# The last stage of a transformer kernel as loops: both expert outputs added to the residual on VectorE

## The reference

```python
logits = jnp.einsum('sbd,de->sbe', x, Wg) + bg + bias
vals, idx = jax.lax.top_k(logits, TOP_K)          # TOP_K = 2
w = jax.nn.softmax(vals - jnp.max(vals, axis=-1, keepdims=True), axis=-1)
cw = jnp.einsum('sbk,sbke->sbe', w, jax.nn.one_hot(idx, NUM_EXPERTS, dtype=x.dtype))
h = jax.nn.relu(jnp.einsum('sbd,edh->esbh', x, W1) + b1[:, None, None, :])
y = jnp.einsum('esbh,ehd->esbd', h, W2) + b2[:, None, None, :]
out = jnp.einsum('esbd,sbe->sbd', y, cw)
...
x = x + _L1_ffn_ref(_layernorm(x, axis=-1), ...)
```

## Time and profile before

| | |
|---|---|
| median of 3 runs | 2008.19 us (2007.45 to 2008.85) |
| the profiled execution | 2008.85 us |
| its span, first to last instruction | 2007.1 us |
| busy, share of the span | PE 87%, DVE 64%, ACT 51%, POOL 23% |
| the edited stage, first load to last instruction | 1967.63 to 2007.1 us |
| loads and stores in it | 16 and 8 of 512 KB |
| the last store is issued at | 2003.76 us |

### The profile page before, as it was taken

How to read it: one execution, slowest core, us unless ns; L and a number is a source line. 1 busy time by engine, 2 the same in 40 slices (tenths; PEclk the granted TensorE clock), 3 DMA queues, 4 the chain that set the end, 5 groups by cost and what they waited for, 6 DMA issues and landing times. The chain is left out here.

```text
span 2007.1 us, 38130 instructions
## 1 busy us (share of the span) xinstructions
PE 1746.5 (87%) x10689; PEld 1076.5 (54%) x10690; DVE 1293.4 (64%) x2730; ACT 1016.1 (51%) x2046; POOL 458.4 (23%) x597
## 2 busy tenths in 40 slices
PE   6949999999999999998869986999978549999990
PEld 5802333233233233222758875989876249988880
DVE  7759888788788788871458868555546662222224
ACT  4614777667677677777235432344322225554442
POOL 4636000000000000000101224322122155555550
PEclk9957999999999999999879997999988759999995
DMA  4562221122221122200010001131311922222117
GB/s 152 162 149 32 33 33 33 35 33 33 35 33 33 35 33 33 33 1 1 0 12 1 0 11 44 44 84 42 85 43 51 339 91 66 65 65 65 63 63 259
DMA packets 119479, 121.80 MB, mean 61 GB/s; under 512 B 20692, under 2 KB 97512, under 8 KB 119208
## 3 DMA queue, kind: packets, MB, share of 16 engines
q1 hardware_dynamic: 106568, 94.35, 19.9%
q0 software_dynamic: 7584, 20.72, 3.2%
q10 hardware_dynamic: 5184, 4.98, 0.7%
HBM read 88.04 MB, written 31.59 MB: 60 GB/s over the span
## 5 line engine op out<-in xcount | busy, mean ns | idle before, releaser
L1873 DVE TENSOR_REDUCE mx<-ps 128x1 f32<-128x512 f32 x1024 | 634.9, 682 | 104.5 <-PE ps L2020 104.2
L1947 ACT ACTIVATE PR<-ps 128x512 f32<-128x512 f32 x1024 | 533.9, 607 | 189.5 <-PE ps L2081 186.1
L2020 PE MATMUL ps<-KQ 96*128 96x512 bf16 x1024 | 408.7, 405 | 34.2 <-PEq L210 25.3
L2081 PE MATMUL ps<-KQ 99*128 99x512 bf16 x1024 | 391.8, 389 | 18.5 <-issue 9.8
L2020 PEld LDWEIGHTS ps<-KQ 96*128 96x128 bf16 x1024 | 99.5, 99 | 360.0 <-DVE mx L1873 270.1
L2046 PE MATMUL ps<-PR,VO 128*32 128x512 f32 x2048 | 270.3, 606 | 0.0
L2081 PEld LDWEIGHTS ps<-KQ 99*128 99x128 bf16 x1024 | 99.7, 98 | 143.7 <-ACT PR L1947 59.2
L1968 POOL COPY VO<-V 128x512 f32 (+1 forms) x16 | 9.8, 615 | 719.8 <-PE ps L2046 719.6
L1746 PEld LDWEIGHTS ps<-e_xinT,e_w 128*128 128x128 f32 x1264 | 156.6, 195 | 5.8 <-issue 1.9
L1746 PE MATMUL ps<-e_xinT,e_w 128*128 128x128 f32 x1264 | 157.5, 279 | 1.1 <-ACT e_xinT L1678 1.1
L1736 PE MATMUL ps<-eW,e_hiddenT 128*128 x632 | 154.9, 388 | 3.1 <-issue 1.1
(11 more groups left out here) (289 smaller groups left out, 2354.0 us busy)
## 6 DMA issues: line engine op xcount, KB each, us to landing
KQ<-qk_parts SPq DMA_DIRECT2D x192, 128.0 KB, 4.7
TB<-toeplitz_lines SPq DMA_DIRECT2D x32, 512.0 KB, 5.9
qk_parts<-parts SPq DMA_DIRECT2D x8, 1536.0 KB, 6.8
eW<-in_L_ffn_W SPq DMA_DIRECT2D x16, 512.0 KB, 6.3
eW<-in_L_ffn_W SPq DMA_DIRECT2D x8, 1024.0 KB, 12.0
e_got<-expert_outputs SPq DMA_DIRECT2D x16, 512.0 KB, 9.7
X<-in_L_attn_x SPq DMA_DIRECT2D x8, 512.0 KB, 4.7
expert_inputs<-e_xn SPq DMA_DIRECT2D x8, 512.0 KB, 3.2
```

What stands on the lines that cost most here:

```text
L1873: nc.vector.reduce_max(mx[:, k, h, q:q + 1], ps[:, bank(r, ("max", t))], AX).then_inc(red_done, 1)
L1947: nc.scalar.activation(PR[:, kt % 2, h, qc * BANK:(qc + 1) * BANK], ps[:, st_bank(r, s)], ACT.Exp).then_inc(exp_done, 1)
L2020: nc.tensor.matmul(ps[:, bank(r, ("max", t))], KQ[r][0:KROWS, 1, h, q * P:(q + 1) * P], KQ[r][0:KROWS, 0, h, k * BANK:(k + 1) * BANK], sta ...
L2081: nc.tensor.matmul(ps[:, st_bank(r, s)], KQ[r][0:AROWS, 0, h, kt * P:(kt + 1) * P], KQ[r][0:AROWS, 1, h, qc * BANK:(qc + 1) * BANK], start ...
```

## The change

The stage's three lists become loops on the engines, and ScalarE no longer computes.

SyncE: a loop of two rounds with four chunks each. It first adds 32 to the semaphore `added`, so that each chunk can wait for a positive number. Each of its two loads (slot 0, then slot 1) has a row number worked out in the loop, and both raise the one semaphore of the buffer.

VectorE: the same loop. For each chunk it waits for its own adds of the chunk before, copies the chunk's 128 x 8 weights into a small buffer `w`, waits for the copy and for both loads, then does four scaled adds for slot 0, waits for these, and does four scaled adds for slot 1. Each add reads and writes the tile X[:, CT*c + k], and its address is worked out in the loop. The buffer `second`, the scalings and the wide add are gone.

ScalarE: a loop of eight rounds, each of which waits for a chunk's eight adds and issues its store.

```diff
@@ -1760,51 +1760,46 @@
         with ExitStack() as s2:
             LOADED = 4
             got = sbuf(s2, "e_got", [P, LOADED, 2, CT, D])
-            second = sbuf(s2, "e_second", [P, 2, CT, D])
-            loaded = [[sem(f"e_y_loaded{r}{s}") for s in range(2)] for r in range(LOADED)]
-            scaled, first_added, added, out_stored = (sem(n) for n in ("e_scaled", "e_first_added", "e_added", "out_stored"))
-            flat = lambda v: v.rearrange("p k d -> p (k d)")
+            w = sbuf(s2, "e_weight", [P, 2, 2, CT])
+            loaded = [sem(f"e_y_loaded{r}") for r in range(LOADED)]
+            load_turn, w_ready, added, out_turn, out_stored = (sem(n) for n in ("e_load_turn", "e_w_ready", "e_added", "out_turn", "out_stored"))
             with nc.Block() as block:
                 @block.sync
                 def _(sp):
-                    for c in range(NC):
-                        r = c % LOADED
-                        if c >= LOADED:
-                            sp.wait_ge(added, c - LOADED + 1)
-                        for s in (1, 0):
-                            rows = y_rows[FREE * P + s * T + CW * c:FREE * P + s * T + CW * (c + 1), :]
-                            sp.dma_start(got[:, r, s], rows.rearrange("(k p) d -> p k d", p=P)).then_inc(loaded[r][s], 16)
+                    sp.sem_inc(added, 2 * CT * LOADED)
+                    with sp.Fori(0, NC // LOADED) as i:
+                        for r in range(LOADED):
+                            c = LOADED * i + r
+                            sp.wait_ge(added, 2 * CT * (c + 1))
+                            for s in range(2):
+                                sp.sem_inc(load_turn, 1)
+                                sp.dma_start(got[:, r, s], y_rows[ds(FREE * P + s * T + CW * c, CW), :].rearrange("(k p) d -> p k d", p=P)).then_inc(loaded[r], 16)
+
+                @block.vector
+                def _(dve):
+                    with dve.Fori(0, NC // LOADED) as i:
+                        for r in range(LOADED):
+                            c = LOADED * i + r
+                            n = 2 * CT * (c + LOADED)
+                            dve.wait_ge(added, n)
+                            dve.sem_inc(load_turn, 1)
+                            nc.vector.tensor_copy(w[:, r % 2], weight[:, :, ds(CT * c, CT)]).then_inc(w_ready, 1)
+                            dve.wait_ge(w_ready, c + 1)
+                            dve.wait_ge(loaded[r], 32 * i + 32)
+                            for s in range(2):
+                                for k in range(CT):
+                                    row = X[:, ds(CT * c + k, 1), :].rearrange("p a d -> p (a d)")
+                                    nc.vector.scalar_tensor_tensor(row, got[:, r, s, k], w[:, r % 2, s, k:k + 1], row, op0=ALU.mult, op1=ALU.add).then_inc(added, 1)
+                                if s == 0:
+                                    dve.wait_ge(added, n + CT)
 
                 @block.scalar
                 def _(act):
-                    def store(c):
-                        act.wait_ge(added, c + 1)
-                        act.dma_start(out_tiles[:, CT * c:CT * (c + 1), :], X[:, CT * c:CT * (c + 1), :]).then_inc(out_stored, 16)
-                    for c in range(NC):
-                        r = c % LOADED
-                        act.wait_ge(loaded[r][1], 16 * (c // LOADED) + 16)
-                        if c >= 2:
-                            act.wait_ge(added, c - 1)
-                        for k in range(CT):
-                            last = nc.scalar.activation(second[:, c % 2, k], got[:, r, 1, k], ACT.Copy, scale=weight[:, 1, CT * c + k:CT * c + k + 1])
-                        last.then_inc(scaled, 1)
-                        if c > 0:
-                            store(c - 1)
-                    store(NC - 1)
+                    with act.Fori(0, NC) as c:
+                        act.wait_ge(added, 2 * CT * (c + 1 + LOADED))
+                        act.sem_inc(out_turn, 1)
+                        act.dma_start(out_tiles[:, ds(CT * c, CT), :], X[:, ds(CT * c, CT), :]).then_inc(out_stored, 16)
                     act.wait_ge(out_stored, 16 * NC)
-
-                @block.vector
-                def _(dve):
-                    for c in range(NC):
-                        r = c % LOADED
-                        dve.wait_ge(loaded[r][0], 16 * (c // LOADED) + 16)
-                        for k in range(CT):
-                            t = CT * c + k
-                            nc.vector.scalar_tensor_tensor(X[:, t], got[:, r, 0, k], weight[:, 0, t:t + 1], X[:, t], op0=ALU.mult, op1=ALU.add).then_inc(first_added, 1)
-                        dve.wait_ge(scaled, c + 1)
-                        dve.wait_ge(first_added, CT * (c + 1))
-                        chunk = flat(X[:, CT * c:CT * (c + 1), :])
-                        nc.vector.tensor_tensor(chunk, chunk, flat(second[:, c % 2]), op=ALU.add).then_inc(added, 1)
 
 
 def attention(nc, sem, stack, sbuf, ps, ident, identb, KQ, kq_loaded, load_qk, V, ffw):
```

## The result

| | kernel before | kernel after |
|---|---|---|
| median of the compared runs, us | 2008.16 (2007.45 to 2008.85, 4 runs) | 2020.19 (2017.67 to 2025.98, 4 runs) |
| span of the profiled execution, us | 2007.1 | 2012.7 |
| end of VectorE's last `e_y` add to the first load | 8.33 | 8.81 |
| first load's issue to the end of the span | 39.5 | 44.9 |

The ratio is 1.0061, 95% interval 1.0044 to 1.0078: slower by 12.0 us in the medians. All 23 executions of after on that chip lie between 2013.85 and 2026.3 us. The profiled one is from their low end (its span is 2012.7 us, theirs go from 2011.9 to 2024.4): it is only 5.6 us longer than the profile of before. So two things have to be explained: what the profile shows, and why most executions are another 3 to 6 us longer. They turn out to be different questions.

A forecast was written before the change was run, and what follows sets the result against it. The bound was to pass from DMA transfers (4.1 us a chunk) to VectorE (4.70); start, first addresses, chunk 0, seven periods and store gave plus 7.0 us on the median 2008.19, so 2015.2 us, range 2009.8 to 2018.5.

The forecast's parts named there:

- Nothing earlier is edited, so only the time from the first load to the end can move: Edited stage is the program's last; only its time was summed, plus 7.0 us in all.
- if the time before 1967.6 differs: Sign of a wrong prediction: a changed time ahead of the edited stage; the other sign was a period under 4.1 or over 5.1.
- The start, 0.4: SyncE's semaphore add, loop entry, wait and address delay the first load by 0.4 us, bounds 0.2 and 0.8.
- Two addresses for each add: VectorE's scaled adds: two address computations, 0.44 us in all, set the spacing; four adds take 1.80 us.
- The drains, 0.25 + 0.40 + 0.30 = 0.95: VectorE's three waits for its own work in each chunk: 0.95 us together, bounds 0.30 and 1.3.
- The period, 4.70: VectorE's time per chunk, 0.95 + 0.15 + 1.80 + 1.80 = 4.70 us, passing the DMA engines' 4.1 us.
- The DMA share: Stage's middle: share near 0.95 instead of 1.09, from 1.573 MB in 4.70 us, 335 GB/s.
- The loads were hidden: Loads into freed slots arrive in time: 2004.5 at the latest, before chunk 7 begins at 2006.6.
- The rule of the Trainium skill: Scaled adds at half throughput: 0.69 us each, period about 6 us, end some 17 us later; given no chance.
- One address for each add: Rival: computed address of X serves both operands; spacing 0.40, period 4.24, plus 3.3 us, 2011.5; chance 0.20.
- More register work: Rival: each add needs one more operation; spacing 0.55, period 5.4, plus 12.3 us, 2020.5; chance 0.11.
- The transfers stay the bound: Rival: VectorE's period at most 4.1 us, so it keeps up with DMA; plus 1.7 us, 2009.9; chance 0.08.

The follow-up runs named there:

- a_again: The kernel after, unchanged, run again against the kernel before: median 2022.48 us against 2008.58, ratio 1.0052.
- d_again: The kernel after, unchanged, run once more against the kernel before in a later set: median 2018.90 us against 2010.42, ratio 1.0047.
- a_vector_loop_only: The kernel after with SyncE and ScalarE written out, only VectorE keeping its loop, against the kernel before: median 2016.86 us against 2008.58, ratio 1.0040.
- a_vector_unrolled: The kernel after with VectorE's list written out, loops kept on SyncE and ScalarE, against the kernel before: median 2015.87 us against 2008.58, ratio 1.0025.
- a_no_loops: The kernel after with the stage written out on all three engines, against the kernel before: median 2010.72 us against 2008.58, ratio 1.0011.

## Why the prediction was wrong in size, point by point

The direction and the mechanism held: slower (0.73 had been given to it), because VectorE becomes the bound. The time did not: 2020.19 us lies above the range's end of 2018.5.

**The step that failed** is "Nothing earlier is edited, so only the time from the first load to the end can move". Its sum was +7.0 us over the median before. The profiled pair gives +5.9 by the same terms, so the sum within the stage was 1.1 too large, not too small. The whole kernel is 8.8±1.4 to 11.0±1.7 us slower in the two repeats and 12.0 in the first medians: 3 to 6 us that the sum had no term for. The stage was 44.9 or 45.0 us in all three profiles of after, so they lie ahead of the first load. The prediction had named this as a sign of being wrong ("if the time before 1967.6 differs"); the first profile, with its first load at 1967.80, did not show it, and the second, at 1976.3, did.

**Within the stage:**
- The start, 0.4: measured 0.48. The two addresses before the first add, 0.20: measured 0.27. The copy has no share in it, since it was over by 1967.96, under the load; from the load's landing to the first add there are 0.31 us (1973.26 to 1973.57), where there were 0.03.
- Two addresses for each add: right, two FUSED_REGOPS of 93 ns. But in place of the two ALU_OP of 40 ns that were taken over from the norm's loop there is one more FUSED_REGOPS of 53 ns, in six of the eight chunks, and the spacing is 0.40 ((1.67 - 0.48) / 3), not 0.44. The sequencer keeps up. This is the one term that was much mis-sized: eight adds take 1.67 + 1.67, not 1.80 + 1.80, and over eight chunks that is 2.1 us. The other way go 0.7 us for drains and copies (with the long gap of the second chunk, below) and 0.2 to 0.3 for the start, the first addresses and the store, which leaves the 1.1.
- The drains, 0.25 + 0.40 + 0.30 = 0.95: measured 0.27 + 0.42 + 0.30 = 0.99. The copy, 0.15: measured 0.17. In the second chunk the gap behind the copy is 0.72, in all six profiles of kernels with attention's loop and this copy in VectorE's loop; in the two with attention written out it is 0.42. What makes that one longer was not found.
- The period, 4.70: measured 4.50, over 4.1, so the verdict "VectorE becomes the bound" held. Cutting the copies took the bound away again. (The prediction read 2 us of idle time before each chunk from chunk 4 on in before; the timeline has 2.14, 1.23, 0.24 and 1.98. The 4.1 us of the transfers do not rest on it.)
- ScalarE's store, +0.2: measured +0.30.
- The DMA share was expected near 0.95 in the middle. It stayed at 1.09 to 1996 and then fell, to a mean of 0.53 to 2009, since the loads ran ahead into their four slots; the mean over both, (24 x 1.09 + 13 x 0.53) / 37 = 0.89, is near the rate that was meant, its course is not.
- The loads were hidden, as said: no gap of a later chunk ends with one, and they landed sooner (7.5 us median, where it was 9.7).
- The rule of the Trainium skill (Vector Engine (DVE) Microarchitecture Reference, "Points that are easy to get wrong"), half throughput for scalar_tensor_tensor with both sources in SBUF and not bf16, is not what the 64 adds show: 480 ns each for 256 columns, 0.40 us apart, against 425 ns for the plain add. The measurement decides; the sum without the rule was right.

**The rivals.** "One address for each add" had foretold 2011.5 by a period of 4.24; the addresses are two, but the spacing of that case came true. "More register work", 2020.5, lies nearest to the median and is wrong all the same: there is one more operation for 36 of the 64 adds, of 53 ns, but no spacing is over 0.40. A time that fits does not make a mechanism right. "The transfers stay the bound" fell with the period of 4.50, and nothing came out faster.

**The time left over.** What is shown: it is no part of the VectorE loop's price, since the three pairs on one chip give 4.7, 5.6 and 6.0 us for that loop, within their errors (1.4 to 2.0) of the 4.9 to 5.2 us in the stage. It does not come with attention's loop alone either: with that written out in both kernels 3.1 us are left over. The profiles are too few to see it. The seven executions with attention's loop and VectorE's loop in the stage had their first load between 1966.3 and 1978.5, 1971.4 in the mean; the nine without VectorE's loop between 1965.9 and 1974.2, mean 1970.3. Single executions scatter by more than what is looked for. The 16 profiles do show where they scatter: line 545's first add, behind the attention, begins between 981.4 and 994.3, and from there to the first load it is 983 to 987 us in every one. What goes with the scatter can be read from each execution's mean granted clock. Over the 23 executions of after on the first chip, time and clock have a correlation of -0.89, and 1.4 us go with each 0.001 of clock; in the 25 of before beside a_again it is -0.82 and 1.3. The mean clock was 0.921 in after and 0.924 in those of before. Clock not granted, (1 - clock) times the span, is 160 us against 153. Of these 7 us the longer stage, at 0.50, explains 2.8; about 4 remain, the size of what is left over there. That is an association, not a cause, and in d_again, where 2.7 us are left over, it does not show (157.0 us not granted against 154.8, less than the stage alone explains), nor in the pair with attention written out (146.7 against 143.7, of which the stage explains all). One at a time, the candidates came out empty: shifted code, idle loops, ScalarE's loop. SyncE's loop has 1.4±0.6 left over in before, yet taking it out of after brought nothing (10.7±1.8). The loops of SyncE and ScalarE together are the one candidate for which the means say something: with both, a_again stands 3.8±2.0 us over a_vector_loop_only, and a_vector_unrolled 3.3±1.7 over a_no_loops, of which the start is 0.5. No run isolates it, and three idle loops cost nothing. So it stays open why the median of after is 3 to 6 us above what its stage costs. Small pieces of 1 to 2 us, each under what 12 executions resolve, would do; so would a lasting effect on the clock that a few profiles cannot show.

## What to carry to other kernels

When work moves from an engine with time to spare to another, cost the waits of that engine on itself first: here busy time rose by 5 us, and 8 x 0.99 us of drains decided. A computed address was free here as long as the sequencer stayed ahead (two for each add, with 0.40 us from add to add), and a small copy with two waits (0.86 us a chunk) was not; move it out of the inner loop. A sum over the edited stage predicts the stage; where single executions scatter by 10 us, give the total a wider range than the sum's own bounds, and repeat a profile before believing a difference ahead of the edit.

## What the runs showed of the hardware that was not expected

- TensorE's compare-and-branch at the end of a long loop body took 4.2 to 5.3 us when it went back, three times in each execution, and 0.083 when it left the loop. With that loop written out, the kernel before takes 18 us less in the median. The three branches last 14.3 us together in before, with gaps of 9.8 us in TensorE's own work behind them; how the 18 divide was not measured, but the mean granted clock of its executions rose from 0.923 to 0.928.
- With that loop written out, the times of before lie within 3.6 us (1989.65 to 1993.22, 5 runs), where 17 executions of before on that chip spread over 11 us (2005.72 to 2016.77). That the spread shrinks is not shown by so few: after with that loop written out spread over 5.3 and 7.3 us in six runs each.
- Two computed operands on VectorE cost two FUSED_REGOPS of 93 ns, and in six of eight chunks a third of 53 ns at k above 0, but no ALU_OP, where one computed operand in the norm's loop had one of 40 ns at k above 0. All of it was hidden: four adds took 1.67 us with 11 such operations, with 8 and with none.
- With computed addresses behind it, a wait of VectorE for its own last instruction cost 0.27 to 0.42 us, where it was 0.10 in before; with the loop written out the same waits and copy fit into a period of 3.74 us in place of 4.50.
